# Graph layers on Trainium2: in the first sum over messages GpSimd takes half of the one-hot rows for the edge tally, and the SP queue takes over GpSimd's reports of arrived tiles

## The chip, the cores and the metric

One core of a Trainium2 chip runs the whole program. The metric is the device time of one execution in microseconds (us), as the median of several runs. Engines are written as the profile writes them: PE (TensorE), DVE (VectorE), ACT (ScalarE), POOL (GpSimd) and SP (SyncE, which only issues transfers and waits). A "q" behind an engine's name (PEldq, DVEq, SPq) is its sequencer, the part that reads registers, waits on semaphores and hands instructions on.

## The reference, cut to what matters

Four graph layers run over 50,000 nodes with 128 features and 50,000 edges; the changed code belongs to the first. Edges are sorted by `dst`, and `dst` is drawn as a square, so that low nodes have many edges and high nodes few.

```python
src = randint(0, 50000);  dst = (50000 * uniform ** 2.0)          # 50000 edges
_o = argsort(dst); src, dst = src[_o], dst[_o]
...
h = leaky_relu(layer_norm(h @ w2 + b2, g2, be2)) * edge_attr[:, None]   # a message per edge
out = segment_sum(h, target, num_segments=N)                            # first sum over messages
...
deg = segment_sum(ones_like(dst), dst, num_segments=n_nodes)            # how many edges end in a node
```

## The kernel before, in words

`aggregate` does a `segment_sum`. It is called six times; the call named `agg0` is the first, right behind `edge_mlp`, which wrote the messages in the order of the edges. It is the only call with `rows_of_edges` None (messages are read as they lie, by whole transfers, not gathered by rows). Nodes lie in 392 tiles of 128 and edges in 392 tiles of 128. The work is a walk of 784 steps: each step adds one edge tile to one node tile, and then moves on either by an edge tile or by a node tile. `setup` works out from `dst` which (`k.places`, `k.needs`, `k.left_i`, `k.done_i`). Four steps make a **round**, so there are 196 rounds; the loop runs 49 times over 4 of them.

In a round of `agg0`:

- SP loads edge tiles in groups of four (256 KB) into `msgs`, a ring of 16 tiles, so four groups. Group g may be loaded when PE has summed the last tile of group g-4 (`summed` against `k.left_i`). A load adds to `gathered{u}` when it lands.
- POOL does nothing but wait for `gathered{u}` and then add 4 to `arrived` (L298).
- DVE reads two numbers of `k.needs` into registers (L367), waits for `arrived` and `ready` (L384), and makes `onehot` (L386): for each of 4 steps a 128x128 matrix that says which edge goes to which row of the node tile. Then, if `tally` is given, it makes for two more edge tiles the one-hot rows of the tally: `hot_lo`, 128 wide (L395), of the node's place in its tile, and `hot_hi`, 392 wide (L396), of its tile. Both have 4 buffers: a round waits until the tally products of four rounds before are done (`tallied`, which PE starts at 4).
- PE waits for `onehot` and sums the four steps into the PSUM bank (L448, each product as two passes, so 8 instructions), reads the places of the next round into registers (L451, two loads), waits for `hot` and multiplies `hot_lo` by `hot_hi` into `counts` (L455, two products).
- ACT empties a node group (L485), refills the bank with the rows of `before` (L472) and issues the store and the next load.

The lead of DVE over PE is bounded by the four buffers of `onehot` and of `hot`. `agg0` and `agg3` have a tally; in `agg3` edges come by gathers that POOL issues. `agg5` has weights, and there SP already reports arrivals itself, in `arrive`, two groups behind its own loads. Every stage ends with a barrier of all engines.

Of the kernel before, what the change touches and what calls it, by code (L numbers as in the profile page):

```python
# [7 lines left out]
ALU = mybir.AluOpType  # L8
ACT = mybir.ActivationFunctionType
AX_X = mybir.AxisListType.X  # L10
ds = bass.ds

P = 128
# [6 lines left out]
STEPS = NT + ET  # L20
Q = 4
# [3 lines left out]
RING = 16  # L25
BANKS = 4
GROUPS = NT // Q
# [225 lines left out]
def aggregate(nc, k, name, table, rows_of_edges, out, before=None, scale=None, tally=None, weights=None, floor=False):  # L253
# [5 lines left out]

    BLOCKS, REST = ET // RING, ET % RING
    ROUNDS = (GROUPS - 2 * BANKS) // BANKS
    whole = rows_of_edges is None or weights is not None
    loads = RING // Q if whole else RING
    sm = phase(nc, name, [f"gathered{j}" for j in range(loads)] + [f"written{u}" for u in range(BANKS)] + [f"before{u}" for u in range(BANKS)]
               + [f"weight{u}" for u in range(RING // Q)] + ["rows", "pass_pool", "pass_dve", "arrived", "hot", "tallied", "tally_c", "tally_to_act", "tally_rooted", "tally_to_pe", "tally_offset", "onehot", "summed", "zeros", "cleared", "ready", "emptied", "weighted"])
    with ExitStack() as ctx:
        def sb(nm, shape, dt=F32):
            return ctx.enter_context(nc.sbuf_tensor(f"{name}_{nm}", shape, dt))  # L270

        msgs = sb("msgs", [P, RING, C])
        onehot = sb("onehot", [P, 4, Q, P])
        kept = sb("kept", [P, BANKS, Q, C])
        if tally is not None:
            hot_lo, hot_hi = sb("hot_lo", [P, 4, 2, P], BF16), sb("hot_hi", [P, 4, 2, NT], BF16)
            counts = ctx.enter_context(nc.psum_tensor(name + "_counts", [P, 512], F32))
            scan, one_row, below, offset = sb("scan", [P, NT]), sb("one_row", [P, NT]), sb("below", [P, P]), sb("offset", [P, 1])
            off = ctx.enter_context(nc.psum_tensor(name + "_off", [P, 512], F32))
        if rows_of_edges is not None:  # L280
            rows = sb("rows", [P, 3, RING], I32)
        if weights is not None:
            weight = sb("weight", [P, RING, HEADS])
# [7 lines left out]
        with nc.Block() as block:  # L291
            @block.gpsimd
            def _(pool):
                if rows_of_edges is None:
                    with pool.Fori(0, GROUPS // (RING // Q)) as i:
                        for u in range(RING // Q):
                            pool.wait_ge(sm[f"gathered{u}"], i * 16 + 16)
                            pool.sem_inc(sm["arrived"], Q)  # L298
                    for u in range(GROUPS % (RING // Q)):
                        pool.wait_ge(sm[f"gathered{u}"], 16 * (GROUPS // (RING // Q)) + 16)  # L300
                        pool.sem_inc(sm["arrived"], Q)
                    return

                def copy_rows(b, third, tiles):
                    nc.gpsimd.tensor_copy(rows[:, third, 0:tiles], rows_of_edges[:, ds(b * RING, tiles)]).then_inc(sm["rows"], 1)  # L305

                def load(b, third, tiles, next_tiles):
                    pool.wait_ge(sm["rows"], b + 1)
                    for c in range(tiles // Q):
                        pool.wait_ge(sm["summed"], pool.value_load(k.left_i[0:1, ds(b * (RING // Q) + c, 1)], min_val=1, max_val=STEPS + SHIFT))  # L310
                        pool.sem_inc(sm["pass_pool"], 1)
                        for j in range(c * Q, c * Q + Q):
                            if weights is not None:
                                pool.indirect_dma_start(weight[:, j, :], None, weights[:, :], bass.IndirectOffsetOnAxis(  # L314
                                    ap=rows[:, third, j:j + 1], axis=0)).then_inc(sm[f"weight{c}"], 16)
                            else:
                                pool.indirect_dma_start(msgs[:, j, :], None, table[:, :], bass.IndirectOffsetOnAxis(  # L317
                                    ap=rows[:, third, j:j + 1], axis=0)).then_inc(sm[f"gathered{j}"], 16)
                        if c == 1 and next_tiles:
                            copy_rows(b + 1, (third + 1) % 3, next_tiles)  # L320

                copy_rows(0, 0, RING)
                with pool.Fori(0, BLOCKS // 3 - 1) as i:
                    for third in range(3):
                        load(i * 3 + third, third, RING, RING)
                for third in range(3):
                    load(BLOCKS - 3 + third, third, RING, RING if third < 2 else REST)
                load(BLOCKS, 0, REST, 0)

            @block.sync  # L330
            def _(sp):
                if whole:
                    def load(i, u):
                        g = i * (RING // Q) + u
                        sp.wait_ge(sm["summed"], sp.value_load(k.left_i[0:1, ds(g, 1)], min_val=1, max_val=STEPS + SHIFT))
                        sp.dma_start(msgs[:, u * Q:(u + 1) * Q, :], rows_of(table, g)).then_inc(sm[f"gathered{u}"], 16)

                    def arrive(i, u):
                        sp.wait_ge(sm[f"gathered{u}"], i * 16 + 16)
                        sp.wait_ge(sm[f"weight{u}"], i * (16 * Q) + 16 * Q)  # L340
                        sp.sem_inc(sm["arrived"], Q)

                    def body(i, u):
                        if live(i, u):
                            load(i, u)
                        if weights is not None and live(*before_by(i, u, 2)):
                            arrive(*before_by(i, u, 2))

                    rounds(sp, body, 2 if weights is not None else 0)
                    return  # L350
                with sp.Fori(0, BLOCKS) as i:
                    for j in range(RING):
                        sp.wait_ge(sm[f"gathered{j}"], i * 16 + 16)
                        sp.sem_inc(sm["arrived"], 1)  # L354
                for j in range(REST):
                    sp.wait_ge(sm[f"gathered{j}"], 16 * BLOCKS + 16)
                    sp.sem_inc(sm["arrived"], 1)

            @block.vector
            def _(dve):  # L360
# [4 lines left out]
                with dve.Fori(0, STEPS // (4 * Q)) as i:  # L365
                    for j in range(4):
# [24 lines left out]
                        if tally is not None:  # L391
                            dve.wait_ge(sm["tallied"], i * 4 + (j + 1))
                            for w in range(2):
                                at = i * 8 + (j * 2 + w)
                                nc.vector.tensor_scalar(hot_lo[:, j, w, :], k.iota[:, 0:P], tally[0][:, ds(at, 1)], None, ALU.is_equal)  # L395
                                last = nc.vector.tensor_scalar(hot_hi[:, j, w, :], k.iota[:, 0:NT], tally[1][:, ds(at, 1)], None, ALU.is_equal)  # L396
                            last.then_inc(sm["hot"], 1)

# [28 lines left out]
            def _(pe):  # L427
# [12 lines left out]
                with pe.Fori(0, STEPS // (4 * Q)) as i:  # L440
                    for j in range(4):
                        slot = [pe.snap(r, min_val=0, max_val=RING - 1) for r in regs[0:Q]]
                        column = [pe.snap(r, min_val=0, max_val=BANKS * Q - 1) for r in regs[Q:2 * Q]]
                        pe.wait_ge(sm["onehot"], i * 4 + (j + 1))
                        if weights is not None:
                            pe.wait_ge(sm["weighted"], i * 4 + (j + 1))
                        for q in range(Q):
                            t.matmul(bank[:, column[q], :], onehot[:, j, q, :], messages[:, slot[q], :], start=False, stop=True, skip_group_check=True)\  # L448
                             .then_inc(sm["summed"], 1)
                        for half in (0, Q):  # L450
                            pe.reg_load(regs[half:half + Q], k.places[0:1, ds(i * 4 + (j + 1), 1), half:half + Q])  # L451
                        if tally is not None:
                            pe.wait_ge(sm["hot"], i * 4 + (j + 1))
                            for w in range(2):
                                last = t.matmul(counts[:, 0:NT], hot_lo[:, j, w, :], hot_hi[:, j, w, :], start=False, stop=True, skip_group_check=True)  # L455
                            last.then_inc(sm["tallied"], 1)
# [87 lines left out]
def before_by(i, u, lag, deep=DEEP):  # L544

    back = -((u - lag) // deep)
    return (i - back if back > 0 else i + -back if back < 0 else i), u - lag + back * deep


def live(i, u, deep=DEEP):  # L550

    return not isinstance(i, int) or 0 <= i * deep + u < GROUPS
# [1303 lines left out]
```

## Time and profile before

| | us |
|---|---|
| median of 3 runs (7369.54 to 7371.06) | 7370.18 |
| the profiled execution's own time | 7368.71 |
| its span, first to last instruction | 7367.0 |
| DVE busy (55% of the span) | 4082.2 |
| PE busy (68%) | 4972.9 |
| POOL busy (59%) | 4310.7 |
| window 1194 to 1620, which is `agg0` | 426.0 |

The profiled execution is 1.47 us under the median of the runs, and 1.7 us of its time lie outside the span. The shares are averages over some fifteen stages with different limits; what the change is worth is read in `agg0`, 5.8% of the span. The profile calls the tiles of every call of `aggregate` `agg_...`, so a stage is found by its window.

### The profile page before, as it was taken

How to read it: one execution, taken by the hardware profiler on the slowest of the kernel's cores; microseconds unless marked ns; L12 is line 12 of the kernel's file. 1: busy time of each engine (PE TensorE's matmuls, PEld its weight loads, DVE VectorE, ACT ScalarE, POOL GpSimd, SP SyncE). 2: the span in 40 equal slices, each digit the busy share in tenths (PEclk: the TensorE clock that was granted, in tenths of full speed). 3: DMA queues.
4: the chain of work that ended last, by engine and by line, in shares of the span. 5: the costliest groups of instructions: out<-in, count | busy, mean ns of one | idle time of the engine just before them, and what ended most of it. 6: DMA issues, size and time to landing. Idle time of an engine off the chain costs nothing. (4 is left out here: it accounts for less than half of the span.)

```text
span 7367.0 us, 135158 instructions
## 1 busy us (share of the span) xinstructions
PE 4972.9 (68%) x26557; PEld 3915.5 (53%) x26558; DVE 4082.2 (55%) x13584; ACT 2784.0 (38%) x6869; POOL 4310.7 (59%) x5032
## 2 busy tenths in 40 slices
PE   3666666779666566986779566766666666415677
PEld 2555554458555465774557465544444444314555
DVE  4555557877323123664775123866666666553568
ACT  1555553237224235781342135931111111101259
POOL 3777771005677677007750776467777777537730
PEclk7777778999658558995899578977777777655789
DMA  1222223559546334883568356932222222213368
GB/s 30 73 73 73 73 73 120 184 191 383 186 128 193 89 96 126 307 279 87 158 190 264 92 165 212 299 118 69 69 67 69 67 69 67 64 36 82 109 198 291
DMA packets 560375, 1016.31 MB, mean 138 GB/s; under 512 B 118514, under 2 KB 127120, under 8 KB 559888
## 3 DMA queue, kind: packets, MB, share of 16 engines
q1 hardware_dynamic: 229424, 419.18, 17.6%
q10 hardware_dynamic: 197568, 359.75, 14.0%
q0 software_dynamic: 133280, 236.29, 12.9%
q8 instruction: 31, 0.51, 0.0%
q14 instruction: 72, 0.59, 0.0%
HBM read 624.60 MB, written 390.17 MB: 138 GB/s over the span
## 5 line engine op out<-in xcount | busy, mean ns | idle before, releaser
L448 PE MATMUL agg_bank<-agg_msgs,agg_onehot 128*128 x7840 | 1496.5, 351 | 706.7 <-DVE agg_onehot L386 572.5
L448 PEld LDWEIGHTS agg_bank<-agg_msgs,agg_onehot 128*128 128x128 f32 x7840 | 1287.8, 249 | 983.2 <-issue 979.1
L386 DVE TENSOR_TENSOR agg_onehot<-iota,rel 128x512 f32<-128x512 f32 x1176 | 814.9, 693 | 1418.6 <-SPq L354 734.8
L317 POOL DMA_INDIRECT agg_msgs<-y,agg_rows x784 | 779.3, 994 | 236.3 <-issue 195.6
L483 ACT ACTIVATE agg_kept<-agg_bank,inv_root 128x128 f32<-128x128 f32 x784 | 224.1, 368 | 708.5 <-PE agg_bank L448 687.8
L483 ACT ACTIVATE agg_kept<-agg_bank,inv_deg 128x128 f32<-128x128 f32 x784 | 224.1, 368 | 697.7 <-PE agg_bank L448 684.0
L448 PE MATMUL agg_bank<-agg_weighted,agg_onehot 128*128 x1568 | 336.6, 384 | 223.7 <-DVE agg_onehot L386 177.3
L1427 PE MATMUL score_pSrc<-ident,score_xs 128*128 128x128 f32 x392 | 154.9, 402 | 488.5 <-issue 357.4
L314 POOL DMA_INDIRECT agg_weight<-weights,agg_rows x392 | 413.5, 1055 | 121.4 <-issue 101.1
L1094 POOL DMA_INDIRECT mlp_xs<-in_x,mlp_rows x392 | 410.5, 1047 | 120.1 <-issue 119.1
L317 POOL DMA_INDIRECT agg_msgs<-near,agg_rows x392 | 388.0, 990 | 117.5 <-issue 96.9
L1400 POOL DMA_INDIRECT by_source<-score_line,score_places x392 | 390.8, 997 | 109.7 <-issue 106.5
L1375 POOL DMA_INDIRECT score_xs<-x,score_rows x392 | 380.3, 970 | 119.8 <-issue 118.8
L1385 POOL DMA_INDIRECT score_xd<-x,score_rows x392 | 389.0, 992 | 104.9 <-issue 90.0
L1104 POOL DMA_INDIRECT mlp_xd<-in_x,mlp_rows x392 | 387.1, 987 | 104.9 <-issue 89.9
L317 POOL DMA_INDIRECT agg_msgs<-h,agg_rows x392 | 379.3, 968 | 117.5 <-issue 96.9
L715 POOL TENSOR_SCALAR l_o<-l_z,l_rstd,l_shift 128x128 f32<-128x128 f32 x196 | 85.7, 439 | 610.7 <-DVE l_shift L760 608.5
L448 PEld LDWEIGHTS agg_bank<-agg_weighted,agg_onehot 128*128 128x128 f32 x1568 | 291.7, 279 | 269.3 <-issue 269.3
L485 ACT ACTIVATE agg_kept<-agg_bank 128x512 f32<-128x512 f32 x196 | 117.0, 597 | 737.1 <-PE agg_bank L448 737.1
L305 POOL COPY agg_rows<-src_row_of 128x16 int32 (+2 forms) x100 | 28.1, 281 | 600.0 <-POOLq L59 599.8
L1122 PE MATMUL mlp_pSrc<-ident,mlp_xs 128*128 128x128 f32 x392 | 143.9, 380 | 347.8 <-DMA mlp_xd<-in_x,mlp_rows 303.4
L1601 DVE CUSTOM_DVE_ANT_0 score_look_sink<-score_look,score_hot_hi 128x392 f32<-128x392 f32 x392 | 222.1, 567 | 271.2 <-PE score_look L1449 268.9
(332 smaller groups left out, 12895.6 us busy)
## 6 DMA issues: line engine op xcount, KB each, us to landing
sums<-agg_kept ACTq DMA_DIRECT2D x490, 256.0 KB
agg_first<-y ACTq DMA_DIRECT2D x196, 256.0 KB
messages<-mlp_m SPq DMA_DIRECT2D x98, 256.0 KB, 2.1
agg_first<-in_x ACTq DMA_DIRECT2D x98, 256.0 KB
agg_msgs<-messages SPq DMA_DIRECT2D x98, 256.0 KB
l_z<-sums SPq DMA_DIRECT2D x98, 256.0 KB
x<-l_o POOLq DMA_DIRECT2D x98, 256.0 KB
near<-l_near_o SPq DMA_DIRECT2D x98, 256.0 KB
```

The costliest lines, as they stand in the source:

```text
L314: pool.indirect_dma_start(weight[:, j, :], None, weights[:, :], bass.IndirectOffsetOnAxis(ap=rows[:, third, j:j + 1], axis=0)).then_inc(sm ...
L317: pool.indirect_dma_start(msgs[:, j, :], None, table[:, :], bass.IndirectOffsetOnAxis(ap=rows[:, third, j:j + 1], axis=0)).then_inc(sm[f"g ...
L386: nc.vector.tensor_tensor(onehot[:, j, :, :], k.iota[:, 0:P].unsqueeze(1).to_broadcast([P, Q, P]), k.rel[:, ds(i * (4 * Q) + j * Q, Q)].un ...
L448: t.matmul(bank[:, column[q], :], onehot[:, j, q, :], messages[:, slot[q], :], start=False, stop=True, skip_group_check=True)\
L483: last = a.activation(kept[:, u, q, :], bank[:, u * Q + q, :], ACT.Relu if floor else ACT.Copy, scale=scale[:, ds(g * Q + q, 1)])
L1094: pool.indirect_dma_start(xs[:, u, q, :], None, x[:, :], bass.IndirectOffsetOnAxis(ap=rows[:, u, 0, q:q + 1], axis=0)).then_inc(sm[f"src{u ...
L1104: pool.indirect_dma_start(xd[:, u, q, :], None, x[:, :], bass.IndirectOffsetOnAxis(ap=rows[:, u, 1, q:q + 1], axis=0)).then_inc(sm[f"dst{u ...
L1375: pool.indirect_dma_start(xs[:, u, q, :], None, x3[:, :], bass.IndirectOffsetOnAxis(ap=rows[:, u, 0, q:q + 1], axis=0)).then_inc(sm[f"src{ ...
L1385: pool.indirect_dma_start(xd[:, u, q, :], None, x3[:, :], bass.IndirectOffsetOnAxis(ap=rows[:, u, 1, q:q + 1], axis=0)).then_inc(sm[f"dst{ ...
L1400: pool.indirect_dma_start(by_source[:, :], bass.IndirectOffsetOnAxis(ap=places[:, u, q:q + 1], axis=0), line[:, u, q, :], None).then_inc(s ...
L1427: t.transpose(pSrc[:, q, :], xs[:, u, q, :], k.ident[:, :])
L1601: v.tensor_tensor_reduce(out=look_sink[:, q, :], in0=look[:, 0:NT], in1=hot_hi[:, u % 2, q, :], scale=1.0, scalar=0.0, op0=ALU.mult, op1=A ...
```

## The change

It touches `agg0` only (the conditions `rows_of_edges is None`). POOL no longer reports arrivals. Each round it waits for `tallied`, copies the two columns of `k.dst_lo` it needs into a small tile `tally_at`, waits for that copy, and makes both `hot_lo` tiles. DVE makes `hot_hi` only. PE waits for `hot_low` beside `hot`. SP reports the arrival of group g-2 behind its load of group g, as it did in `agg5`.

```diff
             def _(pool):
                 if rows_of_edges is None:
-                    with pool.Fori(0, GROUPS // (RING // Q)) as i:
-                        for u in range(RING // Q):
-                            pool.wait_ge(sm[f"gathered{u}"], i * 16 + 16)
-                            pool.sem_inc(sm["arrived"], Q)
...
+                    with pool.Fori(0, STEPS // (4 * Q)) as i:
+                        for j in range(4):
+                            pool.wait_ge(sm["tallied"], i * 4 + (j + 1))
+                            pool.sem_inc(sm["pass_pool"], 1)
+                            nc.gpsimd.tensor_copy(tally_at[:, j, :], tally[0][:, ds(i * 8 + j * 2, 2)]).then_inc(sm["tally_at"], 1)
+                            pool.wait_ge(sm["tally_at"], i * 4 + (j + 1))
+                            pool.sem_inc(sm["pass_pool"], 1)
+                            for w in range(2):
+                                last = nc.gpsimd.tensor_scalar(hot_lo[:, j, w, :], k.iota[:, 0:P], tally_at[:, j, w:w + 1], None, ALU.is_equal)
+                            last.then_inc(sm["hot_low"], 1)
...
                     def arrive(i, u):
                         sp.wait_ge(sm[f"gathered{u}"], i * 16 + 16)
-                        sp.wait_ge(sm[f"weight{u}"], i * (16 * Q) + 16 * Q)
+                        if weights is not None:
+                            sp.wait_ge(sm[f"weight{u}"], i * (16 * Q) + 16 * Q)
                         sp.sem_inc(sm["arrived"], Q)
...
-                        if weights is not None and live(*before_by(i, u, 2)):
+                        if live(*before_by(i, u, 2)):
                             arrive(*before_by(i, u, 2))
-                    rounds(sp, body, 2 if weights is not None else 0)
+                    rounds(sp, body, 2)
...
                             for w in range(2):
                                 at = i * 8 + (j * 2 + w)
-                                nc.vector.tensor_scalar(hot_lo[:, j, w, :], k.iota[:, 0:P], tally[0][:, ds(at, 1)], None, ALU.is_equal)
+                                if rows_of_edges is not None:
+                                    nc.vector.tensor_scalar(hot_lo[:, j, w, :], k.iota[:, 0:P], tally[0][:, ds(at, 1)], None, ALU.is_equal)
                                 last = nc.vector.tensor_scalar(hot_hi[:, j, w, :], k.iota[:, 0:NT], tally[1][:, ds(at, 1)], None, ALU.is_equal)
...
                             pe.wait_ge(sm["hot"], i * 4 + (j + 1))
+                            if rows_of_edges is None:
+                                pe.wait_ge(sm["hot_low"], i * 4 + (j + 1))
```

How a round stands in the instruction streams follows. ISA and REGISTER_ALU are steps of the sequencer. A wait stands with the name under which its semaphore's number was first used in the program, so the names in brackets tell only that there is a wait and on how many semaphores.

On DVE, one round of `agg0` before:

```order
L386 TENSOR_TENSOR agg_onehot<-iota,rel 128x512
L392 REGISTER_ALU
L395 ISA [waits mlp_recip2]
L395 TENSOR_SCALAR agg_hot_lo<-iota,dst_lo 128x128
L396 REGISTER_ALU
L396 TENSOR_SCALAR agg_hot_hi<-iota,dst_hi 128x392
L395 ISA
L395 TENSOR_SCALAR agg_hot_lo<-iota,dst_lo 128x128
L396 REGISTER_ALU
L396 TENSOR_SCALAR agg_hot_hi<-iota,dst_hi 128x392
```

and the same round of the change:

```order
L392 TENSOR_TENSOR agg_onehot<-iota,rel 128x512
L398 REGISTER_ALU
L403 ISA [waits mlp_normed2]
L403 TENSOR_SCALAR agg_hot_hi<-iota,dst_hi 128x392
L403 ISA
L403 TENSOR_SCALAR agg_hot_hi<-iota,dst_hi 128x392
```

Two instructions and two register steps of a round are gone from DVE.

On PE, between the sums of one round and of the next, before:

```order
L451 TENSOR_LOAD places
L451 ISA
L451 TENSOR_LOAD places
L455 MATMUL agg_counts<-agg_hot_hi,agg_hot_lo 128x392 [waits mlp_rooted2]
L455 MATMUL agg_counts<-agg_hot_hi,agg_hot_lo 128x392
```

and of the change:

```order
L458 TENSOR_LOAD places
L458 ISA
L458 TENSOR_LOAD places
L464 MATMUL agg_counts<-agg_hot_hi,agg_hot_lo 128x392 [waits mlp_stats2,mlp_shift2]
L464 MATMUL agg_counts<-agg_hot_hi,agg_hot_lo 128x392
```

PE has as many rows as before; the first tally product carries two waits in place of one.

On SP, one load of a group in the loop of `agg0`, before:

```order
L335 TENSOR_LOAD left_i
L335 ISA x2
L336 ISA [waits mlp_passed]
L336 DMA agg_msgs<-messages 128x512
L335 ISA
```

and of the change:

```order
L340 TENSOR_LOAD left_i
L340 ISA x2
L341 ISA [waits mlp_src1]
L341 DMA agg_msgs<-messages 128x512
L344 ISA
L340 ISA [waits setup_dve]
```

Behind each load SP now stands waiting for the landing of the group two before, and the report goes out behind that load's issue.

## Rows read from the trace of the kernel before

**Rows 1.** Busy time by window, `agg0`; columns named in the row

```profile
core 0: us, PE busy (x) PEld busy (x) DVE busy (x) ACT busy (x) POOL busy (x), PEclk, DMA share, GB/s
1194.00:1620.00 426.00, 312.41 (x1965) 214.20 (x1963) 345.33 (x983) 118.00 (x197) 0.00 (x0) 0.99 0.57 181
```

**Rows 2.** Who waited for whom, PE and DVE, 1200 to 1610

```profile
PE agg_counts L455 <- DVE agg_hot_hi L396: 57.6, 107, 1.2
PE agg_counts L455 <- issue: 31.7, 82, 1.2
DVE agg_onehot L386 <- issue: 30.7, 79, 0.8
DVE agg_onehot L386 <- POOLq L298: 17.1, 29, 1.3
PE agg_bank L448 <- DVE agg_onehot L386: 3.3, 9, 0.4
```

**Rows 3.** Timeline, DVE, the end of `agg0`

```profile
1609.45 0.69 DVE L386 TENSOR_TENSOR agg_onehot<-iota,rel 128x512 f32<-128x512 f32 x1 [0.19 <-issue]
...
1610.79 0.42 DVE L396 TENSOR_SCALAR agg_hot_hi<-iota,dst_hi 128x392 bf16<-128x392 f32 x1
1618.00 0.57 DVE L402 TENSOR_SCALAR degree<-agg_counts 128x392 f32<-128x392 f32 x1 [6.79 <-PE agg_counts L455]
```

**Rows 4.** Timeline, PE, the first round and the last rounds of `agg0`

```profile
1199.07 2.06 PE L448 MATMUL agg_bank<-agg_msgs,agg_onehot 128*128 x8 [3.12 <-DVE agg_onehot L386]
...
1611.52 0.50 PE L455 MATMUL agg_counts<-agg_hot_hi,agg_hot_lo 128*128 128x392 bf16 x2 [0.37 <-DVE agg_hot_hi L396]
...
1613.69 0.50 PE L455 MATMUL agg_counts<-agg_hot_hi,agg_hot_lo 128*128 128x392 bf16 x2 [0.62 <-issue]
1614.08 1.15 PE L448 MATMUL agg_bank<-agg_msgs,agg_onehot 128*128 x8
1615.56 0.50 PE L455 MATMUL agg_counts<-agg_hot_hi,agg_hot_lo 128*128 128x392 bf16 x2 [0.33 <-issue]
1615.98 1.15 PE L448 MATMUL agg_bank<-agg_msgs,agg_onehot 128*128 x8
1617.46 0.50 PE L455 MATMUL agg_counts<-agg_hot_hi,agg_hot_lo 128*128 128x392 bf16 x2 [0.33 <-issue]
```

**Rows 5.** Timeline, DVE, two rounds near the start

```profile
1203.04 0.69 DVE L386 TENSOR_TENSOR agg_onehot<-iota,rel 128x512 f32<-128x512 f32 x1
1203.65 0.28 DVE L395 TENSOR_SCALAR agg_hot_lo<-iota,dst_lo 128x128 bf16<-128x128 f32 x1
1203.85 0.42 DVE L396 TENSOR_SCALAR agg_hot_hi<-iota,dst_hi 128x392 bf16<-128x392 f32 x1
1204.18 0.28 DVE L395 TENSOR_SCALAR agg_hot_lo<-iota,dst_lo 128x128 bf16<-128x128 f32 x1
1204.38 0.42 DVE L396 TENSOR_SCALAR agg_hot_hi<-iota,dst_hi 128x392 bf16<-128x392 f32 x1
1204.81 0.69 DVE L386 TENSOR_TENSOR agg_onehot<-iota,rel 128x512 f32<-128x512 f32 x1
```

**Rows 6.** PE's register loads, 1200 to 1612: count, ns min/median/max

```profile
L451 PEldq TENSOR_LOAD <-places x386: 327/333/1193, 1199.7 to 1611.1; - x193
```

**Rows 7.** SP's loads, POOL's reports (whole span): same columns, first and last start

```profile
L336 SPq FUSED_REGOPS  x176: 46/46/51, 1210.7 to 7071.8; - x176
L336 SPq DMA_DIRECT2D agg_msgs<-messages x98: 327/333/352, 1194.5 to 1593.9; - x98
L336 SPq MOVE agg_msgs<-messages x88: 29/29/29, 1210.8 to 1581.0; - x88
L298 POOLq EVENT_SEMAPHORE  x96: 17/17/17, 1197.8 to 1583.9; - x96
```

**Rows 8.** Timeline, DVE, the first round of `agg0`

```profile
1198.19 0.69 DVE L386 TENSOR_TENSOR agg_onehot<-iota,rel 128x512 f32<-128x512 f32 x1 [8.99 <-POOLq L298]
```

**Rows 9.** POOL's small instructions and one small DVE instruction, by line

```profile
L943 POOL COPY l2b_factor<-root x98: 183/187/217, 4569.5 to 4813.9; 128x4 f32 x80, 128x4 f32<-128x4 f32 x18
L715 POOL TENSOR_SCALAR l_o<-l_z,l_rstd,l_shift x196: 437/439/453, 1632.6 to 1894.6; 128x128 f32<-128x128 f32 x196
L945 POOL TENSOR_TENSOR l2b_res<-l2b_res,l2b_factor x98: 1038/1040/1067, 4569.8 to 4814.2; 128x512 f32<-128x512 f32 x98
L985 DVE SCALAR_TENSOR_TENSOR l2b_shift<-l2b_mv,l2b_rstd x98: 161/164/1032, 4579.4 to 4832.8; 128x4 f32<-128x4 f32 x98
L305 POOL COPY agg_rows<-src_row_of x100: 194/212/729, 1910.8 to 4519.0; 128x16 int32 x84, 128x16 int32<-128x16 int32 x12, 128x8 int32<-128x8 int32 x4
```

More of the change, by code:

```diff
@@ L266, in aggregate @@
     sm = phase(nc, name, [f"gathered{j}" for j in range(loads)] + [f"written{u}" for u in range(BANKS)] + [f"before{u}" for u in range(BANKS)]
-               + [f"weight{u}" for u in range(RING // Q)] + ["rows", "pass_pool", "pass_dve", "arrived", "hot", "tallied", "tally_c", "tally_to_act", "tally_rooted", "tally_to_pe", "tally_offset", "onehot", "summed", "zeros", "cleared", "ready", "emptied", "weighted"])
+               + [f"weight{u}" for u in range(RING // Q)] + ["rows", "tally_at", "hot_low", "pass_pool", "pass_dve", "arrived", "hot", "tallied", "tally_c", "tally_to_act", "tally_rooted", "tally_to_pe", "tally_offset", "onehot", "summed", "zeros", "cleared", "ready", "emptied", "weighted"])
     with ExitStack() as ctx:
@@ L278, in aggregate @@
             scan, one_row, below, offset = sb("scan", [P, NT]), sb("one_row", [P, NT]), sb("below", [P, P]), sb("offset", [P, 1])
+            tally_at = sb("tally_at", [P, 4, 2])
             off = ctx.enter_context(nc.psum_tensor(name + "_off", [P, 512], F32))
@@ L294, in _ @@
                 if rows_of_edges is None:
-                    with pool.Fori(0, GROUPS // (RING // Q)) as i:
-                        for u in range(RING // Q):
-                            pool.wait_ge(sm[f"gathered{u}"], i * 16 + 16)
-                            pool.sem_inc(sm["arrived"], Q)
-                    for u in range(GROUPS % (RING // Q)):
-                        pool.wait_ge(sm[f"gathered{u}"], 16 * (GROUPS // (RING // Q)) + 16)
-                        pool.sem_inc(sm["arrived"], Q)
+                    with pool.Fori(0, STEPS // (4 * Q)) as i:
[8 more added lines that the diff above has]
+                            last.then_inc(sm["hot_low"], 1)
                     return
```

## The prediction

> **What bounds the kernel now.** I read the windows first. `agg0` takes 426 us and in it DVE is busy for 345, PE for 312, POOL for nothing [rows 1]. That looks like a stage bound by DVE, and the view of waits seems to say so: PE waits 57.6 us in front of the tally product for `hot_hi`, which DVE makes [rows 2]. Both are misleading, and the last rounds show it. DVE's last `onehot` starts at 1609.45 and ends at 1610.14, its last `hot_hi` ends at 1611.21, and then DVE sits idle for 6.79 us until PE is done [rows 3]. PE uses that `onehot` at 1615.98 and that `hot_hi` at 1617.46 [rows 4]. So DVE is 5.84 us ahead with the one and 6.25 us with the other, nearly three rounds, which is about what four buffers allow. An engine so far ahead is not waited for: where the view of waits names `hot_hi`, it names the last thing that PE's semaphore saw, not what PE stood for.
>
> What PE does when DVE is silent gives its own pace. The tally products that start at 1611.52, 1613.69, 1615.56 and 1617.46 are 2.17, 1.87 and 1.90 us apart, 1.98 on average [rows 4], with all that they need made long ago. A round over the whole stage is (1617.96 - 1199.07) / 196 = 2.137 us [rows 4]. So PE keeps nearly its own pace all along. What fills the 1.9 us is not arithmetic: 8 passes take 1.15 and the two tally products 0.50, and between them come two register loads, one behind the other, of 333 ns each, some of them far longer (up to 1193) [rows 4, 6]. That is PE's sequencer, and the change takes nothing from it. DVE's own pace is 1.77 us, from one `onehot` at 1203.04 to the next at 1204.81 [rows 5], faster than PE's. It starts with no lead, gains some 0.3 us a round, and then stands at its buffers: hence its waits for PE and for "issue".
>
> **The change part by part.**
>
> *DVE without `hot_lo`.* By starts a round is 0.61 (`onehot`) + 0.20 + 0.33 + 0.20 + 0.43 us [rows 5]; without the two `hot_lo` 0.61 + 0.33 + 0.43 = 1.37. That is 0.40 x 196 = 78 us of DVE's time. On the path it is worth nothing as long as PE needs 2.14, and it is hidden by DVE's lead. If the lead were not there, the gain would be 0.40 a round until PE's own 1.98 is reached: (2.137 - 1.98) x 196 = 31 us, which is the most that this edit can give.
>
> *POOL's work.* POOL has no row of this form in the trace. Per round: a copy of 2 columns, nearest to the copy of 4 columns at 187 ns; then two comparisons of 128x128, nearest to the 128x128 TENSOR_SCALAR at 439 ns [rows 9]. Between copy and comparisons lies a semaphore, some 0.15 us by my estimate. Sum 0.19 + 0.15 + 0.88 = 1.2 us of 2.14, beside PE's work, and started four rounds early. From below, a comparison does less than a multiply and add, and could take no less than the copy, 187 ns; from above, the 128x512 TENSOR_TENSOR at 1040 [rows 9] would give 2.4 us, over the bound. I take 439, since shape and kind are the same. POOL decides the time only from (2.14 - 0.34) / 2 = 0.9 us for each comparison.
>
> *POOL and DVE at the same time.* Some pairs of their instructions hinder each other: a DVE instruction of 161 ns on 4 columns takes up to 1032 while POOL runs its 1040 ns TENSOR_TENSOR, and a POOL copy of 212 takes up to 729 in the sums by gathers, where DVE makes its `onehot` [rows 9]. So POOL can hold DVE for 1032 - 161 = 0.87 of its 1.04 us, all but 0.17, and `onehot` can hold POOL for 729 - 194 = 0.53 of its 0.69. By these rows the new POOL instructions can hold DVE for 0.02 + 2 x 0.27 = 0.56 us a round, so that DVE needs at worst 1.37 + 0.56 = 1.93, still under 2.14. Worth nothing while the lead covers it. If the whole length of every instruction were exclusive, a round would be 0.69 + 2 x 0.42 + 0.19 + 2 x 0.44 = 2.60 us, and the stage (2.60 - 2.137) x 196 = 91 us longer.
>
> The Trainium skill states just that (SBUF — State Buffer, section "Who interferes with whom"): a DVE instruction with two SBUF inputs, or one in a 2-port mode, and a GpSimd instruction exclude each other, and the lock is held for the whole instruction. By that rule the sum would be the 2.60 us and 91 us; that they exclude each other agrees with the 1032 ns of [rows 9], but that nothing of an instruction's time is free of it does not.
>
> *PE's second wait.* It rides on the same instruction: PE's rows are as many as before. Nothing. If it cost one more step of a sequencer, that would be 0.05 x 196 = 10 us (SP's smallest such step takes 46 ns [rows 7]).
>
> *SP's report.* This is the term that costs. POOL reported a group as it landed. Now group g is reported behind SP's load of g+2, and that load waits until PE has summed the last tile of g-2. From that sum to PE's use of group g the chain is: SP's wait, move and issue, 46 + 29 + 333 ns [rows 7], with some 0.15 between them and the report, 0.57; from the report (1197.8) to the start of `onehot` (1198.19), 0.4 [rows 7, 8]; `onehot` 0.69; from its end, 1198.88, to PE, 1199.07, 0.19 [rows 4, 8]. Together 1.85 us. PE has, where group g-1 fills just the round between, one round of 1.90 less what was left of the round in which g-2 ended. If that is the first step, PE has 1.90 - 0.35 = 1.55; if the second or third, 1.30 or 1.05 (a step is about a quarter of 1.15). The stalls are 0.3, 0.55, 0.8 us. If it is the fourth step, a full round lies between and none arises.
>
> How often that is follows from `dst`. The steps that `setup` works out from it: of the 98 groups 14 are as tight as that, all among the first 34, where a node tile has many edge tiles: 9 times the first step, 4 times the second, once the third. 9 x 0.3 + 4 x 0.55 + 0.8 = 5.7 us. Later a group of four edge tiles goes with four and more node tiles, lasts 2 to 3 rounds, and the report comes in good time. In the early rounds the loss of lead is also where POOL can touch the path: `onehot` comes when POOL is in its second comparison, at most 0.27 us for 9 rounds, 1.5 us taken. Against it stand the waits for `onehot` that were there before, 3.3 us in all [rows 2], of which I take off 1. Sum: +6 us. Bounds: 0, if the chain is shorter than 1.55; 14 x 0.8 + 34 x 0.27 = 20 us, if every tight group is hit as the worst.
>
> **Sum.** Against the profiled execution's 7368.7: 0 + 0 + 0 + 6 = 7374.7. The runs' median is 1.5 higher, so 7376.2.
>
> **The rivals.**
>
> *DVE was the bound after all* (faster). For: 345 us busy, and the 57.6 us in the waits. Against: 6 us of lead. It gives up to 31 us: 7339. 7%.
>
> *PE's register loads get shorter* (faster). The longer ones (up to 1193 ns against 333 [rows 6]) must come from something else that loads or issues at the time. DVE's own load of `needs` comes earlier in the round by some 0.25 us when two instructions and their steps are gone, and may fall clear of PE's. Rounds at 1.98 throughout would again be 31 us. It can as well fall onto them, so half of it is the likelier end: 7355. 5%.
>
> *POOL and DVE take turns and become the bound* (slower; ends on the other side). Place: `onehot` and `hot_hi` on DVE against three POOL instructions, in every round. From the point where DVE or POOL needs over 2.14 us a round it decides, for all 196 rounds. For: the 1032 and 729 ns. Against: 1.93 at worst by those rows. Half way between 1.93 and 2.60 gives 2.27, or 26 us: 7396. 10%. Beside it the rule of whole instructions, 2.60: 7461, 4%.
>
> By the page of the Trainium skill named above it would be this last case.
>
> *A comparison on POOL takes over 0.9 us* (slower). 1.0 us would make a round 0.34 + 2.0 = 2.34 and the stage 40 us longer: 7410. 4%.
>
> **How the numbers follow.** A measurement of this kernel can tell about 0.2%, 14.7 us, from no change. The forecast, +6 within 0 and 20, has 70%, and nearly all of it lies within 0.2%; I move 2 of these 70 to slower. Faster: 7 + 5 = 12, less 1 for cases that end under 0.2%: 11. Slower: 10 + 4 + 4 + 2 = 20. Same: 69. For the range I leave out the DVE rival below and the three dearest cases above: 7352 to 7404. The forecast's own range is 7368 to 7392.
>
> **What the profile of the change would show.** DVE's two `hot_lo` rows gone in `agg0`, its busy time there down from 345 to about 240 us (two of 0.28 a round). POOL with 196 copies and 392 comparisons, near 0.19 and 0.44 us. PE's products as dense as before, rounds of 2.13 to 2.14 after the first fifty, and DVE still idle for 5 us and more before `degree`. In the first forty rounds PE waiting for `onehot`, some 0.3 to 0.8 us at a time, and DVE for SP's report. Some `onehot` or `hot_hi` longer than 0.69 and 0.42. Wrong would be: DVE finishing less than 2 us ahead of PE (the turns), comparisons of 0.9 us, or fewer long register loads on PE.

## The result, and the profile after

The change is slower: the median of 12 runs is 7392.09 us (7377.17 to 7402.1) against 7369.38 us for the kernel before on the same chips (12 runs, 7358.76 to 7377.92). The ratio is 1.0033, interval 1.0025 to 1.0040. That is 22.7 us more, where 6 were forecast; the profiled execution has a span of 7390.9 us, 23.9 more than before.

Nearly all of it lies in `agg0`. The stage is measured from the first product that clears PE's bank to `degree`, which waits for the last tally product. The rows of the clearing products by tile, with count, ns min/median/max, first and last start, of the kernel before and then of the changed one:

```profile
L430 PE MATMUL agg_bank<-zeros_b x4: 581/629/629, 1193.8 to 1195.0; 1*128 1x512 bf16 x4
```

```profile
L437 PE MATMUL agg_bank<-zeros_b x4: 581/626/627, 1194.7 to 1195.9; 1*128 1x512 bf16 x4
```

`degree` starts at 1618.0 before [rows 3] and at 1642.0 after (timeline below). That is 424.2 us before and 447.3 us after, 23.1 more. The window of just that stretch of the changed kernel answers to [rows 1]:

```profile
1194.70:1642.00 447.30, 315.54 (x1965) 220.76 (x1965) 281.03 (x589) 117.46 (x196) 344.59 (x588) 0.98 0.54 172
```

DVE has lost the work that was moved. Over the same stretch it was busy for 343.5 us before and is for 281.0 now. That is 62.5 us less, not the 105 that the prediction took from two rows of 0.28 a round, since those overlap their neighbours. By starts the moved work is 78 us; some 13 us of it came back, because `onehot` and `hot_hi` became longer (707 and 444 ns on average, for 693 and 418). POOL now has 345 us. PE's work is nearly the same (312.6 us before, 315.5 now, at a mean granted clock of 0.99 and 0.98), so what grew is mostly PE's idle time, from 111.6 to 131.8 us.

Is PE waited on by someone late? The end of the stage on DVE and PE, by timeline (start, us, what, idle before), answers to [rows 3, 4]:

```profile
1632.75 0.69 DVE L392 TENSOR_TENSOR agg_onehot<-iota,rel 128x512 f32<-128x512 f32 x1 [0.51 <-PE agg_bank L455]
...
1641.98 0.57 DVE L409 TENSOR_SCALAR degree<-agg_counts 128x392 f32<-128x392 f32 x1 [7.73 <-PE agg_counts L464]
```

```profile
1635.25 0.49 PE L464 MATMUL agg_counts<-agg_hot_hi,agg_hot_lo 128*128 128x392 bf16 x2 [0.48 <-issue]
...
1637.46 0.49 PE L464 MATMUL agg_counts<-agg_hot_hi,agg_hot_lo 128*128 128x392 bf16 x2 [0.67 <-issue]
...
1639.44 0.49 PE L464 MATMUL agg_counts<-agg_hot_hi,agg_hot_lo 128*128 128x392 bf16 x2 [0.44 <-issue]
...
1641.45 0.49 PE L464 MATMUL agg_counts<-agg_hot_hi,agg_hot_lo 128*128 128x392 bf16 x2 [0.44 <-issue]
```

DVE idles 7.73 us before `degree` where it idled 6.79, so at the end it is still over three rounds ahead. But PE's own rounds, with nothing left to wait for, have become longer: 2.21, 1.98 and 2.01 us between starts where they were 2.17, 1.87 and 1.90 [rows 4], and the gap before the last two tally products is 0.44 where it was 0.33. That is about 0.1 us a round. PE's sequencer has a row that it did not have:

```profile
L462 PEldq EVENT_SEMAPHORE  x196: 51/51/51, 1201.8 to 1641.3; - x196
```

L462 is the wait for `hot_low`. It is a step of its own, 51 ns long, where the kernel before has no such row for its one wait in the same place.

The row of POOL's comparisons by line:

```profile
L305 POOL TENSOR_SCALAR agg_hot_lo<-iota,agg_tally_at x392: 594/602/1270, 1195.5 to 1635.1; 128x128 bf16<-128x128 f32 x196
```

A comparison takes 0.60 us at the median, not the 0.44 taken for it. The copies (L301) take 175 to 688 ns, so both kinds are stretched at times to twice and more. The groups by line, with shapes, from 1200 to 1640 (busy us, mean ns of one, idle time before them) give the means:

```profile
L305 POOL TENSOR_SCALAR agg_hot_lo<-iota,agg_tally_at 128x128 bf16<-128x128 f32 x386 | 286.7, 753 | 42.2 <-POOL agg_tally_at L301 42.2
...
L403 DVE TENSOR_SCALAR agg_hot_hi<-iota,dst_hi 128x392 bf16<-128x392 f32 x392 | 158.3, 444 | 0.0
L392 DVE TENSOR_TENSOR agg_onehot<-iota,rel 128x512 f32<-128x512 f32 x196 | 138.6, 707 | 163.1 <-SPq L347 79.4 <-PE agg_bank L455 52.4 <-issue 15.7
L464 PE MATMUL agg_counts<-agg_hot_hi,agg_hot_lo 128*128 128x392 bf16 x390 | 97.9, 332 | 106.1 <-issue 62.0 <-DVE agg_hot_hi L403 37.4 <-POOL agg_hot_lo L305 6.6
```

The stretching comes from DVE. By the starts and ends in the trace, the 88 comparisons with no `onehot` or `hot_hi` of DVE beside them took 0.60 us on average and 0.61 at the most; the 77 that met a `hot_hi` alone took 0.76.

### The profile page after: what moved, and what is told of

Its sections match the earlier page's. It is cut to its first block and busy times, and to the rows that moved or that the text cites. A ratio compares the mean times of both kernels' runs of the same rounds, so it can differ in the third digit from the quotient of the medians.

```text
span 7390.9 us, 136108 instructions
## 1 busy us (share of the span) xinstructions
PE 5002.6 (68%) x26557; PEld 3940.7 (53%) x26558; DVE 4014.0 (54%) x13192; ACT 2783.0 (38%) x6869; POOL 4654.5 (63%) x5620
## 5 line engine op out<-in xcount | busy, mean ns | idle before, releaser
L1436 PEld LDWEIGHTS score_pSrc<-ident,score_xs 128*128 128x128 f32 x392 | 78.1, 199 | 508.4 <-issue 508.2
```

The costliest lines, as they stand in the source:

```text
L1436: t.transpose(pSrc[:, q, :], xs[:, u, q, :], k.ident[:, :])
```

## The experiments

Each run is compared with runs of the kernel before on the same chip. "Stage" is the stretch from the first clearing product to `degree`, in the one profiled execution; before it is 424.2 us. The stages of e4 and e5, which change nothing in the time, lie within 1 us of that. Outside the stage the same code differs more from one execution to the next (the profiled executions of e1 and e3 spend 10 and 9 us more there than that of before), so small costs are read from the stage.

| run | median us | beside before | ratio, interval | stage us |
|---|---|---|---|---|
| the change | 7392.09 | 7369.38 | 1.0033, 1.0025 to 1.0040 | 447.3 |
| e1, before with a second wait on PE | 7396.42 | 7373.05 | 1.0030, 1.0019 to 1.0041 | 442.0 |
| e2, the change, wait on DVE | 7382.45 | 7373.05 | 1.0013, 1.0004 to 1.0022 | 431.4 |
| e3, before with SP's reports | 7378.82 | 7373.05 | 1.0007, 0.9998 to 1.0016 | 431.7 |
| e4, before without `hot_lo` | 7371.28 | 7373.05 | 0.9999, 0.9990 to 1.0008 | 425.2 |
| e5, e2 with the report first | 7371.01 | 7371.34 | 1.0001, 0.9992 to 1.0010 | 424.5 |
| e6, before with one register load | 7281.06 | 7371.34 | 0.9880, 0.9865 to 0.9895 | 378.3 |
| e7, e5 with one register load | 7320.30 | 7371.34 | 0.9936, 0.9922 to 0.9949 | 409.5 |
| e8, e2 with POOL's comparisons twice | 7590.38 | 7371.34 | 1.0304, 1.0290 to 1.0318 | 643.9 |
| e9, e7 with half of `hot_lo` on POOL | 7288.16 | 7366.28 | 0.9895, 0.9878 to 0.9911 | 376.5 |
| e10, e6 without `hot_lo` | 7281.31 | 7366.28 | 0.9882, 0.9866 to 0.9899 | 376.0 |

**e1: the second wait alone, in the kernel before.**

```diff
                             pe.wait_ge(sm["hot"], i * 4 + (j + 1))
+                            if rows_of_edges is None:
+                                pe.wait_ge(sm["onehot"], i * 4 + (j + 1))
```

> The kernel before with one thing added: in the first sum PE waits, ahead of the tally products, for one more semaphore (onehot, which it has waited for already, so it is never kept waiting). Theory: the second wait is a step of its own on PE's sequencer, 51 ns and some 50 ns of gap, and PE's sequencer paces the stage; 0.10 us x 196 rounds = 20 us slower than before. Rival (the time went to POOL's and DVE's turns on SBUF, or to the late reports): no change, within 4 us.

Measured: 23 us slower, the stage 17.8 us longer. The semaphore is one that PE has already passed, so nobody can be late for it; POOL, DVE and SP do what they did before. PE's last round shows the same gap as the change's:

```profile
1636.29 0.49 PE L457 MATMUL agg_counts<-agg_hot_hi,agg_hot_lo 128*128 128x392 bf16 x2 [0.45 <-issue]
```

So the second wait alone explains the larger part of the change's loss: 17.8 us of its stage's 23.1, or 0.09 us a round.

**e2: the change, with the wait moved off PE.** DVE waits for `hot_low` ahead of `hot_hi`, so that `hot` vouches for both halves.

```diff
                             dve.wait_ge(sm["tallied"], i * 4 + (j + 1))
+                            if rows_of_edges is None:
+                                dve.wait_ge(sm["hot_low"], i * 4 + (j + 1))
...
                             pe.wait_ge(sm["hot"], i * 4 + (j + 1))
-                            if rows_of_edges is None:
-                                pe.wait_ge(sm["hot_low"], i * 4 + (j + 1))
```

> The change, with the wait for hot_low moved from PE to DVE, ahead of hot_hi, so that hot covers both. Theory: PE's rounds fall back to 1.90 us at best, 20 us come back, and 4 to 6 us over before remain (late reports). Rival (POOL's work itself costs): it stays 20 us over before, or gets worse, since DVE now waits for POOL.

Measured: 16 us of the stage come back (447.3 to 431.4), and 7.2 over before remain. POOL does the same work as in the change, so it is not POOL's work that cost the 16 us.

**e3: SP's reports alone, in the kernel before.** POOL's loop is left out and SP's `arrive` runs as in the change; DVE makes both halves.

```diff
-                        if weights is not None and live(*before_by(i, u, 2)):
+                        if live(*before_by(i, u, 2)):
                             arrive(*before_by(i, u, 2))
-                    rounds(sp, body, 2 if weights is not None else 0)
+                    rounds(sp, body, 2)
```

> The kernel before, with only the reports of arrivals moved from POOL to SP, behind the load of two groups later; POOL idle in the stage, DVE makes both halves. Theory: 4 to 6 us over before, all lost in the first 50 rounds, where PE waits for onehot. Rival (the reports are in time everywhere): 0.

Measured: 5.8 us over before by the runs, with an interval that only just takes in no change, and 7.4 us by the stage (7.45 before rounding). The waits of PE for `onehot` from 1205 to 1300 (us in total, times, longest) tell where. Of the kernel before:

```profile
PE agg_bank L448 <- DVE agg_onehot L386: 1.8, 5, 0.4
```

The same view of e3:

```profile
PE agg_bank L442 <- DVE agg_onehot L380: 5.8, 13, 0.8
```

Thirteen waits of up to 0.8 us: the prediction had 14, of 0.3 to 0.8. In this window they are 4.0 us more than before. The change has 13 such waits and 5.0 us. Where the rest of the 7.4 us lies is shown behind e5.

**e4: no `hot_lo` at all.** The kernel before, but DVE makes no `hot_lo` in `agg0` (it is zero throughout), so the tally of edges is missing from the result.

```diff
                             for w in range(2):
                                 at = i * 8 + (j * 2 + w)
-                                nc.vector.tensor_scalar(hot_lo[:, j, w, :], k.iota[:, 0:P], tally[0][:, ds(at, 1)], None, ALU.is_equal)
+                                if rows_of_edges is not None:
+                                    nc.vector.tensor_scalar(hot_lo[:, j, w, :], k.iota[:, 0:P], tally[0][:, ds(at, 1)], None, ALU.is_equal)
```

> The kernel before, but DVE makes no hot_lo in the first sum (it is set to zero once), so the tally of edges is left out of the result; every wait is as before. Theory: DVE has 78 us less to do and the time stays as before, within 4 us, since PE's sequencer sets the pace. Rival (DVE was the bound): up to 31 us faster.

Measured: no change, and a stage of 425.2 us. The work that the change moves is worth nothing on DVE, even if nobody does it. DVE only waits more: 0.54 us for PE ahead of its last `onehot` (timeline), where the kernel before, with `hot_lo` in its rounds, paused for 0.19 [rows 3].

**e5: e2, and SP reports before it loads.**

```diff
+                        if weights is None and live(*before_by(i, u, 2)):
+                            arrive(*before_by(i, u, 2))
                         if live(i, u):
                             load(i, u)
-                        if live(*before_by(i, u, 2)):
+                        if weights is not None and live(*before_by(i, u, 2)):
                             arrive(*before_by(i, u, 2))
```

> The change with the wait for hot_low on DVE, and SP reports group g-2 ahead of its load of group g, so that the report waits only for the landing. Theory: the early stalls go and the time is that of before, within 4 us; the stage is 424 us as before. Rival (the late reports are not what is left, or SP now loads later because it waits for landings first): 5 to 9 us over before as with the wait on DVE alone.

Measured: the time of before, the stage at 424.5. PE's waits for `onehot` from 1205 to 1300, in the view shown for e3, are down to two, 0.9 us in all.

With both of its costs mended, the move of `hot_lo` to POOL is free and brings nothing. It is free by a small margin only: POOL is busy for 362 of the 424.5 us, stands 42 us between its copies and comparisons, and waits for PE for no more than 13.

**Where along the stage the time is lost.** The table takes the start of the first tally product of a round, counted from the run's own first clearing product, and subtracts the same start in the kernel before (us).

| run | round 21 | round 41 | round 99 | `degree` |
|---|---|---|---|---|
| e1, second wait alone | 2.8 | 4.6 | 10.2 | 17.8 |
| e3, SP's reports alone | 4.6 | 7.4 | 7.8 | 7.4 |
| e2, the change without the second wait | 4.7 | 7.1 | 7.8 | 7.2 |
| the change | 5.4 | 9.6 | 15.5 | 23.1 |
| e5, without both | 0.5 | 0.6 | 0.7 | 0.3 |

The two costs have different shapes. The late reports cost all of their 7 us in the first 41 of 196 rounds and nothing later; the second wait goes on costing to the end. In the change the second wait adds only 2.5 us to e2 by round 41, where it costs 4.6 alone: part of it passes while PE stands waiting for a late report. That is why the change loses 23.1 us and not 17.8 + 7.4 = 25.2.

**e6: one register load of eight numbers in place of two of four, on PE, in all six sums.**

```diff
-                        for half in (0, Q):
-                            pe.reg_load(regs[half:half + Q], k.places[0:1, ds(i * 4 + (j + 1), 1), half:half + Q])
+                        pe.reg_load(regs, k.places[0:1, ds(i * 4 + (j + 1), 1), 0:2 * Q])
```

> The kernel before, with PE's two register loads of four numbers each per round made one load of eight, in all six sums. Theory: PE's sequencer paces the first sum, so a load and its gaps (0.4 us) less per round shortens it until DVE's 1.77 us a round holds it: from 2.13 to about 1.8, 60 us in the first sum, and DVE is the bound then. More in the other sums where PE is the pace. Rival (a load of eight takes as long as two of four, or PE was not the pace): 0 to 10 us.

Measured: 90 us faster, 46 of them in `agg0`. This beats both kernels. The load by line, over the stage:

```profile
L450 PEldq TENSOR_LOAD <-places x196: 587/593/1532, 1199.7 to 1570.8; - x196
```

A round goes from 2.16 to 1.93 us (stage over 196), 46 us in all. The load itself is 593 ns against 2 x 333 [rows 6]; all loads of the stage, summed from the trace, took 154.5 us before and 142.3 here, 12 us less. Each load has a register step of 51 ns ahead of it, and one of two is gone, which is another 10 us. The other 24 us must be gaps around the load that is gone; no run parts them further.

The expectation was too high (60 us in the stage), and its account of where the gain would end was wrong: DVE does not become the bound at 1.8. It comes near, though. Ahead of `degree` it now idles 1.38 us, where it idled 6.79:

```profile
1572.13 0.56 DVE L402 TENSOR_SCALAR degree<-agg_counts 128x392 f32<-128x392 f32 x1 [1.38 <-PE agg_counts L454]
```

What DVE's work still costs at that lead is shown by e10.

**e7: e5 with the one register load.**

> The kernel of the run with the report ahead of the load, and PE's one register load of eight as well. Theory: with PE at 1.5 to 1.6 us a round, DVE at 1.4 and POOL at about 1.7 (copy 0.3, two comparisons of 0.6, a semaphore between), the move of hot_lo is worth something now: the first sum at about 1.7 us a round, 10 to 25 us less than with one load alone. Rival (POOL and DVE hinder each other, or POOL becomes the bound near 2 us): no better than one load alone, or worse.

Measured: 31 us of stage more than e6, and 39 by the runs. Here the rival was right: POOL is the bound. In the whole stage it waits for PE once, for 2.7 us, and it makes its 196 copies at 2.08 us from start to start on average, (1600.3 - 1195.4) / 195. The row by line, and one of the quicker rounds (1.94 us) by timeline:

```profile
L301 POOL COPY agg_tally_at<-dst_lo x196: 174/401/673, 1195.4 to 1600.3; 128x2 f32 x196
```

```profile
1401.70 0.40 POOL L301 COPY agg_tally_at<-dst_lo 128x2 f32 x1
1402.31 1.39 POOL L305 TENSOR_SCALAR agg_hot_lo<-iota,agg_tally_at 128x128 bf16<-128x128 f32 x2 [0.20 <-POOL agg_tally_at L301]
1403.64 0.41 POOL L301 COPY agg_tally_at<-dst_lo 128x2 f32 x1
```

A pair of comparisons takes 1.39 where one alone is 0.60, and the copy 0.40 where its shortest is 0.174: beside a DVE that works at the same time POOL's instructions stretch. What was hidden behind a slow PE becomes the bound with a quick one.

**e8: e2, each comparison on POOL made twice, the first into a tile that nobody reads.**

```diff
+                            for w in range(2):
+                                nc.gpsimd.tensor_scalar(tally_sink[:, j, w, :], k.iota[:, 0:P], tally_at[:, j, w:w + 1], None, ALU.is_equal).then_inc(sm["sunk"], 1)
                             for w in range(2):
                                 last = nc.gpsimd.tensor_scalar(hot_lo[:, j, w, :], k.iota[:, 0:P], tally_at[:, j, w:w + 1], None, ALU.is_equal)
                             last.then_inc(sm["hot_low"], 1)
+                            pool.wait_ge(sm["sunk"], i * 8 + (2 * j + 2))
```

> The change with the wait for hot_low on DVE, and POOL makes each comparison twice (the first into a tile nobody reads). Theory: POOL then needs 0.3 + 0.2 + 4 x 0.6 = 2.9 us a round, over PE's 2.13, and paces the stage: (2.9 - 2.13) x 196 = 150 us slower than before. This gives the point from which POOL decides. Rival (POOL's rows are longer than the work, since it waits for DVE in them): clearly less, 50 to 100 us.

Measured: 219 us slower, the stage at 643.9, 3.29 us a round. The theory had the mechanism and 150 us; it took 0.6 us for a comparison, and beside DVE they took 0.74 to 0.75 on average. The rival was wrong. The window of the stage:

```profile
1195.00:1839.00 644.00, 478.85 (x1965) 325.14 (x1965) 312.78 (x589) 117.46 (x196) 598.71 (x980) 0.66 0.37 119
```

POOL is busy for 93% of it. PE's mean granted clock was 0.66 where it was 0.98 in the change, and its products took 479 us in place of 316. That did not add to the 219 us. The only thing that POOL waits for from another engine is PE's tally product, ahead of each copy, and by line, from 1204 to 1830, the copies had no idle time before them (the last number):

```profile
L301 POOL COPY agg_tally_at<-dst_lo 128x2 f32 x191 | 34.3, 179 | 0.0
```

So POOL set the pace throughout, and the slower products were hidden behind it.

**e9 and e10: what `hot_lo` is worth with a quicker PE.** In e9 POOL makes one of the two comparisons of a round and DVE the other (`for w in (1,)` on POOL, `or w == 0` in DVE's condition). e10 is e6 with `hot_lo` left out as in e4, so again without the tally.

> The kernel with one register load, the report ahead of the load and the wait on DVE, but POOL makes only the second of the two hot_lo of a round, and DVE the first. Theory: POOL now needs 0.3 + 0.2 + 0.7 = 1.2 us a round and DVE 1.77 - 0.20 = 1.57, so neither stands at 1.94 as POOL did with both; the first sum lasts 345 to 375 us, 5 to 30 us less than with one load alone (378). Rival (what POOL takes of the shared accesses costs DVE as much as it saves, or PE is the pace again near 1.9): 375 to 395 us, no gain.

> One register load, and no hot_lo at all in the first sum (set to zero once, so the tally is left out of the result). It shows what hot_lo costs at most once PE's sequencer is quicker. Theory: DVE at 1.37 us a round leaves PE at 1.5 to 1.7: the first sum at 310 to 350 us. Rival (PE is still the pace at 1.9, not DVE): 370 to 380 us, as with one load alone.

Measured: stages of 376.5 and 376.0 us against e6's 378.3, and no gain in time. The theory was wrong in both, the rival right. Even with no `hot_lo` at all, when DVE stands idle for 6.35 us before `degree`, the stage is only 2.3 us shorter:

```profile
1570.81 0.57 DVE L406 TENSOR_SCALAR degree<-agg_counts 128x392 f32<-128x392 f32 x1 [6.35 <-PE agg_counts L458]
```

So PE's sequencer is the pace in e10, at 1.92 us a round, and leaving `hot_lo` out of e6 takes no more than 2.3 us off the stage.

## Why the prediction was right or wrong

*PE's sequencer is the bound, DVE is not: right.* e4 and e10 show it for DVE, e1 and e6 for the sequencer: a step more lengthens the stage, a load less shortens it. The 57.6 us that PE is said to wait for `hot_hi` [rows 2] are not there to be won. The same view of the change names POOL's `hot_lo` as what PE waited for, 6.6 us in all, while e1, without POOL's part, has the same gaps. A lead read from the last rounds is the better witness.

*PE's second wait, costed at nothing: wrong, and this is the step that failed.* The prediction said that the wait "rides on the same instruction", from the order of instructions, in which a wait stands in brackets behind the instruction that it precedes. The trace shows a step of its own, 51 ns, and nearly as much again in gaps. The alternative in the same paragraph, 0.05 x 196 = 10 us, had the mechanism but little more than half its size, since it took the length of the step without the gap. Measured: 17.8 us of stage in e1 (0.09 us a round), 15.9 between the change and e2.

*SP's late reports, +6 us: right in mechanism, place and size.* 13 waits of up to 0.8 us from 1205 to 1300; 5.8 us by the runs of e3, 7.4 by its stage, where 6 were forecast. The table behind e5 has all of it lost by round 41. e5 takes the cost away by the order of two calls. DVE waited for SP's reports much longer than PE lost by them, 79.4 us in the change where it was 17.1 for POOL's before [rows 2], but after the first rounds its lead covers those waits: its `hot_hi` was ready 4.0 us ahead of the tally product in the median round, and 6.4 before.

*DVE's relief, worth nothing: right*, in the change and, to within 2.3 us of stage, in all its variants. Its size was misread in the list of signs: DVE's busy time was to fall to about 240 us, from two whole rows of 0.28 a round, where the prediction's own starts give 78 us less. It fell to 281.

*The rival of shorter register loads did not come true.* The long ones stayed: 66 of the 394 loads of the change's stage took over 1.3 times the median, 70 before.

*POOL's comparison, 0.44 us: off.* It took 0.60 at the least, and 753 ns on average in the change. The nearest row in shape and kind was 27% too short, and the bounds of 187 and 1040 held it. It cost nothing here, because POOL's work lies beside PE's. But the margin was far smaller than the sum had it: POOL was put at 1.2 us of 2.14 a round, and it took 345 / 196 = 1.76 busy and 0.2 between copy and comparison, about 2.0 of 2.28. The point from which POOL decides was put at 0.9 us for each comparison with PE at 2.14; e7, at 0.76 for each and PE quicker, lies past its own point.

*The turns of POOL and DVE: present, and without effect in the change.* `onehot` took 707 ns on average in place of 693, `hot_hi` 444 in place of 418, and DVE still idled 7.73 us before `degree`. The rule of whole instructions from the Trainium skill (SBUF — State Buffer, section "Who interferes with whom") would have made a round of 2.60 us and the stage 91 us longer. With the comparisons of 0.60 as measured, it would be even more. The stage grew by 23.1, and e1, e3 and e5 give the reason for all of that elsewhere. That the two engines hinder each other, as the Trainium skill says, the stretched rows show (594 to 1270 ns); that the time of a round is the sum of whole instructions they do not: e7's round of 2.09 us is under 0.69 + 2 x 0.42 + 0.18 + 2 x 0.60 = 2.91.

*The chances.* The forecast was +6, within 0.2%, with 69%; slower by more had 20%, and no rival named the mechanism that made it so. The one of them that was nearest in time (turns, +26 us) was not what happened. The wide range, 7352 to 7404, holds the 7392.09 by luck: its upper part was there for the turns, and the sum's own terms end at +20 us, where 22.7 were measured.

## What to carry to other kernels

Where an engine's sequencer sets the pace, count its steps and not only its work. Here a second wait (e1) and a register load (e6) each cost their own length and a gap, and the wait cost this although what it waited for was always ready. Put such a wait on an engine that runs ahead and let that one's semaphore vouch for both, as e2 does. And before work is moved off an engine, leave it out altogether in one run: if that gains nothing (e4), no move will, and what remains to be asked is only what the move costs. Ask it again when the pace changes: the same move was free at 2.16 us a round (e5) and cost 31 us of stage at 1.93 (e7).

## What the runs showed of the hardware that was not expected

- A wait on a semaphore on PE's sequencer beside another on the same instruction: a step of 51 ns, and 0.09 us in the round (e1).
- A register load of eight numbers took 593 ns where two of four took 333 each; with the steps around them the round became 0.23 us shorter (e6).
- A comparison on POOL that met no `onehot` or `hot_hi` of DVE took at most 0.61 us; one that met a `hot_hi` alone took 0.76 on average in the change.
- A 128x128 comparison from f32 to bf16 took POOL 0.60 us, against 0.44 for a multiply and add of the same size in f32.
- With POOL as the bound (e8) PE's mean granted clock over the stage was 0.66, with 443 of 644 us at the lower of its two levels (1.2 and 2.4 GHz); with PE as the pace, in the change, it was 0.98, with 19 us at the lower.
